# Inverse square roots of the query and key lengths: from one GpSimd power to a VectorE seed and ten GpSimd Newton operations

## What is computed

```python
def l2norm(t):
    return t / jnp.clip(jnp.linalg.norm(t, axis=-1, keepdims=True), 1e-12)

def _layer(x, wqkv, qs, ksc, wo, lg, lb, w1, b1, w2, b2):
    h = shift_token(x)
    q, k, v = jnp.split(h @ wqkv, 3, axis=-1)      # 8 heads of 64
    q = l2norm(q) * qs
    k = l2norm(k) * ksc
    q, k = rotary_xpos(q, k)
    x = x + local_attention(q, k, v) @ wo          # windows of 64, this one and the one before
    ...                                            # layer norm, gated feed-forward
```

## Time and profile before

| | |
|---|---|
| median of 3 runs | 968.1 us (965.94 to 968.76) |
| the profiled execution's own time | 966.96 us |
| its span, first to last instruction | 965.0 us |
| busy: PE, DVE, ACT, POOL | 786.4, 668.0, 659.3, 539.6 us |
| chain that ended last, by engine | PE 40%, DVE 20%, ACT 19%, issue 11%, POOL 9% |
| POOL's power on 128x32 | 32 of them, 5438 ns each, 174.0 us |
| mean granted TensorE clock | 0.942 |

### The profile page before, as it was taken

The page is one execution under the profiler, slowest core; times in us unless marked ns, Lnnn a source line. Parts: engine busy times, 40 slices in busy tenths (PEclk is TensorE's granted clock), DMA queues, the critical chain, the costliest instruction groups (busy, mean ns, idle before and its releaser), DMA issues.

```text
span 965.0 us, 19306 instructions
## 1 busy us (share of the span) xinstructions
PE 786.4 (81%) x7151; PEld 556.3 (58%) x7151; DVE 668.0 (69%) x1588; ACT 659.3 (68%) x1545; POOL 539.6 (56%) x324
## 2 busy tenths in 40 slices
PE   4456788879889989888969979888888989888874
PEld 4334566656556666655657656656565666656543
DVE  4566876685687877586887967486787776676732
ACT  0234766867576985877786886877675887868672
POOL 2046853493956653394985643293966690576600
PEclk9668789999899999999999999999999999999997
DMA  6000000000000000000000000000000000000000
GB/s 206 0 12 1 12 2 1 1 1 2 1 2 1 23 2 22 2 1 1 1 1 2 23 1 23 1 2 1 1 1 2 12 2 13 2 1 2 1 1 22
DMA packets 12275, 9.85 MB, mean 10 GB/s; under 512 B 1040, under 2 KB 11288, under 8 KB 12184
## 3 DMA queue, kind: packets, MB, share of 16 engines
q1 hardware_dynamic: 12184, 8.64, 3.0%
HBM read 6.54 MB, written 2.10 MB: 9 GB/s over the span
## 4 chain that ended last, share of the span: by engine, by line
PE 40%; DVE 20%; ACT 19%; issue 11%; POOL 9%; DMA 0%; SPq 0%; POOLq 0%; ACTq 0%; DVEq 0%
ACT probs L964 7%; PE pair L696 6%; PE mixed L727 5%; POOL qk L1494 4%; PE dense L831 4%; PE pair L759 3%; DVE space L1393 3%; DVE q_norm L1398 3%; PE dense L795 3%; PE dense L796 2%; PE dense L797 2%; DVE qk L1195 2%; PE dense L908 2%; ACT squares L1083 2%; ACT probs_t L972 2%
## 5 line engine op out<-in xcount | busy, mean ns | idle before, releaser
L1494 POOL TENSOR_TENSOR qk<-space 128x512 f32<-128x512 f32 x128 | 186.4, 1463 | 58.0 <-DVE q_norm L1398 55.1
L1454 POOL TENSOR_TENSOR root<-power,minus_half 128x32 f32<-128x32 f32 x32 | 174.0, 5438 | 4.6 <-DVE power L1404 4.6
L964 ACT ACTIVATE probs<-pair,neg_max 128x128 f32<-128x128 f32 x512 | 138.3, 402 | 18.9 <-DVE neg_max L1215 18.5
L1393 DVE TENSOR_TENSOR space<-dense,tables 128x512 f32<-128x512 f32 x128 | 87.5, 684 | 36.9 <-ACT space L1087 35.2
L908 PE MATMUL dense<-wq_hi,h_hi 128*128 128x512 f32 x192 | 90.2, 470 | 26.6 <-DVE space L1393 10.9
L1491 POOL TENSOR_TENSOR space<-space,tables 128x512 f32<-128x512 f32 x64 | 82.7, 1293 | 50.7 <-ACT space L1087 50.7
L696 PE MATMUL pair<-eye_s,probs 128*128 128x128 f32 x512 | 80.9, 292 | 34.9 <-ACT probs L964 34.7
L1215 DVE TENSOR_REDUCE neg_max<-pair 128x4 f32<-128x512 f32 x128 | 82.0, 684 | 35.2 <-PE pair L759 35.1
L1083 ACT ACTIVATE squares<-dense 128x512 f32<-128x512 f32 x128 | 79.1, 618 | 39.5 <-PE dense L910 38.6
L696 PEld LDWEIGHTS pair<-eye_s,probs 128*128 128x128 f32 x512 | 59.1, 146 | 56.2 <-ACT probs L964 51.9
L1398 DVE TENSOR_REDUCE q_norm<-squares 128x8 f32<-128x512 f32 x128 | 86.4, 675 | 0.0
(11 more groups left out here) (166 smaller groups left out, 1809.2 us busy)
## 6 DMA issues: line engine op xcount, KB each, us to landing
x_in<-n_L_attn_embeddings_dram SPq DMA_DIRECT2D x8, 256.0 KB, 3.0
out_dram<-hn SPq DMA_DIRECT2D x8, 256.0 KB, 2.4
qk<-in_L_ffn_wqkv_dram SPq DMA_DIRECT2D x1, 1536.0 KB, 6.2
qk<-in_L_ffn_w_dram SPq DMA_DIRECT2D x1, 682.0 KB, 7.5
wo_s<-in_L_ffn_wo_dram SPq DMA_DIRECT2D x2, 256.0 KB
o_t<-in_L_wmod_dram SPq DMA_DIRECT2D x1, 384.0 KB, 3.3
probs<-const_rotary_dram SPq DMA_DIRECT2D x1, 256.0 KB, 3.6
band_s<-const_band_dram SPq DMA_DIRECT2D x1, 256.0 KB, 7.8
```

The costliest lines, as they stand in the source:

```text
L964: last = act.activation(probs[:, ring, hh, :], banks[m][:, hh * P:(hh + 1) * P], ACT.Exp, bias=neg_max[:, ring, hh:hh + 1], scale=1.0)
L1393: dve.tensor_tensor(turned_s[:, t % 2, m, :].rearrange("p (h a b) -> p h a b", h=HEADS, a=2), halves[:, :, ::-1, :], rot(layer, t, 2 * m + 1),
L1454: return pool.tensor_tensor(to, of, minus_half[:, 0:of.shape[-1]], ALU.pow)
L1494: pool.tensor_tensor(qk[s][:, t, m * INNER:(m + 1) * INNER], turned_c[:, t % 2, m, :], turned_s[:, t % 2, m, :], ALU.add).then_inc(added, 1)
```

## The change

Three things change. `power` and `root` become two buffers each, taken in turn by pair (`powers`, `roots`; each of `roots` has two rows of 32, `y` and `z`). DVE's step `proj.rsqrt` now writes half of the squared length, waits for that instruction, and makes a first guess of the inverse root with integer arithmetic on the bits of the float. POOL's power gives way to three Newton rounds, ten small operations on 128x32 (two of them on 128x64), each behind a wait for the one before it. `y` ends as the inverse root; `z` is `y` times the half and is carried along, so that a round needs no square. The layer norms' small powers stay. Third, all lists in `ORDER` are written anew.

```diff
-        power, root, scratch = sb("power", [P, 32]), sb("root", [P, 32]), sb("scratch", [P, 1])
+        powers, roots = sb("powers", [P, 2, 32]), sb("roots", [P, 2, 2, 32])
+        scratch = sb("scratch", [P, 32])
+        threes = sb("threes", [P, 32])
...
                     if t % 2 == 0 and m == 0 and past(2 * before + t // 2):
-                        dve.wait_ge(qk_powered, 2 * before + t // 2)
+                        dve.wait_ge(half_set, 2 * before + t // 2)
...
                     dve.wait_ge(summed, 4 * pair_ + 4)
-                    dve.tensor_scalar(power[:, :], q_norm[:, :], 1e-24, None, ALU.max).then_inc(qk_powered, 1)
+                    half, seed = powers[:, pair_ % 2, :], roots[:, pair_ % 2, 0, :]
+                    if past(pair_ - 1):
+                        dve.wait_ge(qk_ready, pair_ - 1)
+                    dve.tensor_scalar(half, q_norm[:, :], 1e-24, 0.5, ALU.max, ALU.mult).then_inc(half_set, 1)
+                    dve.wait_ge(half_set, pair_ + 1)
+                    dve.tensor_scalar(seed.bitcast(I32), half.bitcast(I32), -0.5, RSQRT_SEED, ALU.mult,
+                                      ALU.add).then_inc(qk_seeded, 1)
...
             def unit_root(pair_):
 
-                pool.wait_ge(qk_powered, pair_ + 1)
-                inverse_root(root[:, :], power[:, :]).then_inc(qk_rooted, 1)
+                both, half = roots[:, pair_ % 2, :, :], powers[:, pair_ % 2, :]
+                y, z = both[:, 0, :], both[:, 1, :]
+                count = NEWTON * pair_ + 1
+                pool.wait_ge(qk_seeded, pair_ + 1)
+                pool.tensor_tensor(z, y, half, ALU.mult).then_inc(qk_newton, 1)
+                pool.wait_ge(qk_newton, count)
+                for k in range(3):
+                    pool.tensor_tensor(scratch[:, :], y, z, ALU.mult).then_inc(qk_newton, 1)
+                    pool.wait_ge(qk_newton, count + 1)
+                    pool.tensor_tensor(scratch[:, :], threes[:, :], scratch[:, :], ALU.subtract).then_inc(qk_newton, 1)
+                    pool.wait_ge(qk_newton, count + 2)
+                    if k < 2:
+                        pool.tensor_tensor(both, both, scratch[:, :].rearrange("p (o h) -> p o h", o=1)
+                                           .broadcast_to([P, 2, 32]), ALU.mult).then_inc(qk_newton, 1)
+                        count = count + 3
+                        pool.wait_ge(qk_newton, count)
+                    else:
+                        pool.tensor_tensor(y, y, scratch[:, :], ALU.mult).then_inc(qk_rooted, 1)
```

(`threes` holds 1.5.) Of `ORDER`, one line of POOL's list for turn 1 before and the lines that take its place:

```diff
-        1:ff.stats 1:a.rsqrt 2:new.stats 1:ff.hi 1:proj.split 2:new.steps 1:proj.tile.0.0 1:proj.tile.0.1
+        0:proj.tile.1.1 0:proj.rsqrt.0 0:proj.tile.2.0 0:proj.tile.2.1 0:proj.tile.3.0 1:ff.stats 1:a.rsqrt
+        0:proj.tile.3.1 1:ff.hi 2:new.stats 1:proj.split 1:proj.tile.0.0 2:new.steps 1:proj.tile.0.1
```

More of the change, by code:

```diff
@@ L53 @@
         2:new.turn 2:proj.tile.0.0 2:proj.tile.0.1 2:proj.tile.0.2 2:proj.tile.1.0 2:proj.tile.1.1
[L54 to L57, removed]
@@ L65 @@
[L65 to L69, removed]
@@ L70 @@
[L70 to L74, removed]
@@ new lines @@
+        3:proj.tile.2.1 3:new.turn 3:a.score.2 3:proj.tile.2.2 3:ff.stats 3:a.out.1 3:proj.tile.3.0
+        3:a.turn.3 3:a.score.3 3:a.flip.2 3:new.dots 3:a.mix.2 3:a.flip.3 3:a.mix.3 3:a.out.2 3:ff.norm
+        >0:a.turn.0 3:new.mix 3:a.out.3 3:proj.tile.3.1 >0:a.turn.1 3:proj.tile.3.2 3:new.sum 3:a.project
+        3:ff.up.0 3:ff.up.1 3:ff.up.2 3:ff.down"""),
+        steps("""
+        0:a.score.0 <3:store.turn 0:ff.stats 0:a.score.1 0:a.flip.0 0:a.mix.0 0:a.out.0 0:a.flip.1
+        <3:new.stream 0:ff.norm 0:a.mix.1 0:a.turn.2 0:a.out.1 0:ff.up.0 0:ff.up.1 0:ff.up.2 0:ff.down
@@ new lines @@
+        2:proj.tile.0.2 2:proj.tile.1.0 2:a.score.2 2:proj.tile.1.1 2:proj.tile.1.2 2:proj.tile.2.0
+        2:a.turn.3 2:proj.tile.2.1 2:ff.stats 2:a.score.3 2:proj.tile.2.2 2:a.flip.2 2:new.mix
+        2:proj.tile.3.0 2:a.flip.3 2:a.mix.2 2:a.mix.3 2:proj.tile.3.1 2:ff.norm 2:proj.tile.3.2 2:a.out.2
+        2:a.out.3 2:new.sum 2:ff.up.0 2:ff.up.1 3:a.turn.0 3:a.turn.1 2:a.project 2:new.stream 2:ff.up.2
+        2:ff.down 3:a.score.0 3:a.score.1 2:store.turn 3:proj.tile.0.0 3:proj.tile.0.1 3:a.flip.0
@@ L240 @@
         steps("""
[L241 to L244 removed]
+        2:new.stats 2:proj.split 2:new.turn 2:proj.tile.0.0 2:proj.tile.0.1 2:proj.tile.1.0 2:proj.tile.1.1
@@ new lines @@
+        2:a.mix.0 2:proj.tile.1.0 2:proj.tile.1.1 2:a.mix.1 2:new.dots 2:new.sims 2:proj.rsqrt.0
+        2:proj.tile.2.0 2:new.weights 2:a.score.2 2:proj.tile.2.1 2:ff.stats 2:a.score.3 2:proj.unit.0
+        2:ff.norm 2:proj.tile.3.0 2:a.mix.2 2:proj.tile.3.1 2:a.mix.3 2:ff.hi 2:new.gate 2:proj.rsqrt.1
+        2:new.again 2:new.stream 2:ff.up.0 2:ff.up.1 2:ff.up.2 2:a.project 3:a.unit 2:ff.down 3:proj.split
+        2:store.turn 2:proj.keep 3:a.score.0 3:proj.tile.0.0 3:proj.tile.0.1 3:a.score.1 3:a.mix.0
@@ new lines @@
+        3:proj.tile.1.0 3:new.stats 3:proj.tile.1.1 3:proj.rsqrt.0 3:new.turn 3:proj.tile.2.0
+        3:proj.tile.2.1 3:a.mix.1 3:ff.stats 3:a.score.2 3:ff.norm 3:proj.unit.0 3:a.score.3 3:a.mix.2
+        3:new.dots 3:new.sims 3:a.mix.3 3:proj.tile.3.0 3:new.weights 3:proj.tile.3.1 3:ff.hi 3:proj.rsqrt.1
+        3:new.gate 3:new.again 3:ff.up.0 3:ff.up.1 3:new.stream 3:ff.up.2 3:a.project 3:ff.down >0:a.score.0
+        3:store.turn 3:proj.keep"""),
+        steps("""
+        0:ff.stats 0:a.score.1 0:a.mix.0 0:ff.norm 0:a.unit 0:ff.hi 0:a.mix.1 0:ff.up.0 0:ff.up.1 0:ff.up.2
@@ new lines @@
+        2:new.gate 2:proj.rsqrt.1 2:ff.up.0 2:ff.up.1 2:new.again 2:new.stream 2:ff.up.2 3:a.unit
+        3:proj.split 2:ff.down 3:a.score.0 2:store.turn 3:a.score.1 2:a.project 3:proj.tile.0.0
+        3:proj.tile.0.1 3:proj.tile.1.0 3:proj.tile.1.1 3:a.mix.0 3:proj.rsqrt.0 3:proj.tile.2.0
+        3:proj.tile.2.1 3:a.mix.1 2:proj.keep 3:proj.unit.0 3:proj.tile.3.0 3:a.score.2 3:ff.stats
+        3:a.score.3 3:ff.norm 3:a.mix.2 3:proj.tile.3.1 3:a.mix.3 3:ff.hi >0:a.score.0 3:ff.up.0 3:ff.up.1
```

507 lines of the change are left out of this document (247 added, 260 removed).

## The result

The change made the kernel slower: 978.36 us median (974.43 to 980.21, 6 runs) against 966.82 for the kernel before beside it, ratio 1.0111 with a 95% interval of 1.0094 to 1.0128. The forecast was 959.5 us, with 950 to 970 as the range. The profiled execution took 978.97 us, its span 977.1.

The account below looks back on a forecast made before the run. No engine is full; 7 of POOL's 32 powers lie on the chain and PE waits for POOL. A gain capped at 12.1 us, less 2.5 for the seed and 1.7 for the port, is 7.9: 959.5 us, range 950 to 970.

Parts of the forecast that it names:

- The other moves: Remaining reorderings in the lists, on PE and ACT mostly by one to three places: counted at nothing.
- the cap: PE's waits that POOL ends, without the last layer's feed-forward, limit the gain to 12.1 us instead of 15.8.
- The two moves that were priced: `root_n` behind `h_lo` on POOL, 1.9 us; DVE's pair multiplication behind the gate's first product, 1.65 us; together 3.5.
- The root: POOL's ten small operations take 3.64 us against the power's 5.40; 7 roots on the chain gain 12.3 us.
- Rival 3: Small POOL operations have a fixed cost of some 0.4 us, so the kernel is slower, 972.3 us; chance 0.13.
- The seed: One more DVE instruction for each of 32 pairs, 8.6 us of DVE, of which 0.29 counts: 2.5 us lost.
- Rival 4: DVE's small steps and seeds are each held up for a whole streaming POOL operation, 0.92 us: 964 us; chance 0.07.
- The port's 1.7 us: 41 small DVE steps inside POOL's powers each meet a Newton operation, 0.14 us apiece: 1.7 us lost.

Follow-up runs that it names:

- e1: The change (seed on VectorE, Newton operations on POOL) with the lists of the kernel before: 964.25 us, ratio 0.9958 to the kernel before.
- e3: The kernel before with VectorE's seed instruction added, its result unused, and POOL's power waiting for it: 975.54 us, ratio 1.007 to the kernel before.

## Why the prediction was wrong

- **"The other moves ... I count at nothing: they fill what was idle, and nothing shows their worth."** This is the step that failed. The lists as a whole, priced at a gain of 3.5 us that the cap then swallowed, cost 14.9. PE waits 23.1 us for attention rows where it waited 4.2, though which waits make up the 14.9 stays open. That a move fills idle time was assumed, with no look at what else needs the place it takes. Most moves are short, but in turn 1 `new.mix` goes nine places forward on PE, and VectorE's first tile of slot 2 behind four attention steps.
- **The two moves that were priced, 3.5 us.** `h_lo` did take 1.27 us, and `root_n` did go behind it. But the forecast took both as time saved on POOL's chain, and that chain now waits 5.42 us for VectorE. `h_lo` ends 0.65 us later than before. PE's wait for it, forecast at 5 us or less, is 10.6.
- **The root: right.** 0.25 us on 32 elements, 0.32 on 64, a gap of 0.08, 3.33 us in all; the forecast had 0.27, 0.34, 0.08 and 3.64. Worth 12.3 us by the sum, 10.9 by e1 and e3, if the two add. Rival 3 (small operations are dear) had the right sign with the wrong mechanism: the pitch is 0.33 us where it needed 0.48.
- **The seed: 2.5 us forecast, 6.8 measured.** The share of a VectorE microsecond that reaches the end was not the error: e3 has 30.7 us more of VectorE (698.7 against the earlier trace rows) and is 6.8 longer, a share of 0.22 where 0.29 was taken. Its duration was, 0.77 us instead of 0.27. The mean of the maximum was taken for the seed as well, but the seed comes 0.2 us later, when the POOL add that the same sum releases has begun. Rival 4 had this mechanism for the seeds, at 0.92 us each; the rows give 0.96 to 1.08, for about half of them.
- **The port's 1.7 us** for VectorE's other small steps was not measured by itself. It is inside the 10.9 that is left for the root, which would be larger by it.
- **Without the lists** the sum would have been the same, 12.1 - 2.5 - 1.7 = 7.9 us, since the cap holds for the roots' 12.3 too; e1 measured 4.1. The sign of that half was right, and its miss is the seed's; that of the change was decided by the lists, most of which got no price.
- **The cap of 12.1 us** did not decide anything: what was left of POOL's part came out below it, and PE's waits for POOL did not go.
